# A mixture-of-experts layer: the shared expert's up products ahead of the expert loop, its down products behind it

## What is computed

```python
scores = softmax(xt @ router_w + router_b) + router_bias          # top 2 of 16, out of the best 2 of 4 groups
y = sum over the 16 experts of gate_e * ((silu(xt @ w1 + b1) * (xt @ w2 + b2)) @ w3 + b3)     # 512 -> 128 -> 512
z = silu(xt @ sw1 + sb1) * (xt @ sw2 + sb2) @ sw3 + sb3                                       # 512 -> 256 -> 512
out = x + y + z
```

## Time and profile before

| | |
|---|---|
| median of three runs | 253.63 us (250.83 to 255.41) |
| the profiled execution | 253.11 us, its span 251.4 us |
| busy: TensorE, VectorE, GpSimd, ScalarE | 240.5, 140.5, 110.1, 78.4 us |
| chain that ended last | TensorE 85%, VectorE 10% |
| granted clock of TensorE, mean | 0.993 |

### The profile page before, as it was taken

How to read it: one execution, slowest core, us unless ns; L and a number is a source line. 1 busy time by engine, 2 the same in 40 slices (tenths; PEclk the granted TensorE clock), 3 DMA queues, 4 the chain that set the end, 5 groups by cost and what they waited for, 6 DMA issues and landing times.

```text
span 251.4 us, 3931 instructions
## 1 busy us (share of the span) xinstructions
PE 240.5 (96%) x1092; PEld 162.8 (65%) x1093; DVE 140.5 (56%) x287; ACT 78.4 (31%) x169; POOL 110.1 (44%) x137
## 2 busy tenths in 40 slices
PE   7979999999999889999999999999999999999694
PEld 6847777888764446677777777777777644444231
DVE  0597876489799793333333333333333301698982
ACT  2345555222274002333333333333333311111400
POOL 6696665100200463666666666666663330000710
PEclk9999999999999999999999999999999999999979
DMA  6999998892449479754555444554553216999753
GB/s 198 343 415 404 369 317 304 296 372 59 197 154 417 183 197 330 266 169 168 167 167 167 126 156 135 167 167 167 167 167 125 89 57 232 391 387 389 303 207 126
DMA packets 20699, 57.91 MB, mean 230 GB/s; under 512 B 2533, under 2 KB 2533, under 8 KB 20428
## 3 DMA queue, kind: packets, MB, share of 16 engines
q1 hardware_dynamic: 15084, 39.89, 43.4%
q0 software_dynamic: 5600, 17.83, 21.5%
HBM read 40.94 MB, written 17.30 MB: 232 GB/s over the span
## 4 chain that ended last, share of the span: by engine, by line
PE 85%; DVE 10%; issue 2%; DMA 1%; ACT 0%; DVEq 0%
PE psum L586 76%; PE psum L732 6%; DVE xT L1214 3%; PE psum L629 2%; PE psum L745 2%; DVE xT L980 1%; DVE xT L954 1%; DMA xT<-cond_pack 1%; DVE x_early L954 1%; DVE r L954 1%; DVE xT L994 0%; DVE mix_bias L982 0%; DVE r L1170 0%; DVE code_f L1148 0%; DVE late_region L954 0%
## 5 line engine op out<-in xcount | busy, mean ns | idle before, releaser
L586 PE MATMUL psum<-wexp,r 128*128 x272 | 68.4, 381 | 0.4 <-DVE r L1170 0.3
L586 PEld LDWEIGHTS psum<-wexp,r 128*128 128x128 f32 x272 | 48.5, 190 | 22.8 <-issue 16.8
L954 DVE TENSOR_TENSOR r<-psum,ebias 128x256 f32<-128x256 f32 x34 | 14.4, 425 | 64.5 <-PE psum L586 64.5
L497 POOL DMA_INDIRECT expert_rows<-late_region,to_row x33 | 33.3, 1010 | 33.6 <-ACT late_region L897 33.6
L491 POOL DMA_INDIRECT late_region<-xt_rows,from_row x36 | 35.3, 980 | 16.9 <-issue 10.5
L586 PE MATMUL psum<-wexp,xt_sb 128*128 x68 | 34.8, 594 | 0.0
L586 PE MATMUL psum<-xT,shared_sb 128*128 128x512 f32 x64 | 28.0, 593 | 0.0
L891 ACT ACTIVATE r<-r 128x128 f32<-128x128 f32 x34 | 10.5, 309 | 55.3 <-DVE r L954 55.3
L897 ACT ACTIVATE late_region<-psum 128x512 f32<-128x512 f32 x34 | 20.3, 598 | 15.8 <-PE psum L586 15.8
L1170 DVE COPY r<-psum 128x512 f32<-128x512 f32 x36 | 24.5, 681 | 0.0
L732 PE MATMUL psum<-ident,late_region 128*128 128x128 f32 x144 | 21.6, 273 | 0.9 <-DMA late_region<-xt_rows,from_row 0.9
(11 more groups left out here) (177 smaller groups left out, 303.7 us busy)
## 6 DMA issues: line engine op xcount, KB each, us to landing
wexp<-expert_pack SPq DMA_DIRECT2D x16, 768.0 KB, 6.1
wexp<-expert_rows SPq DMA_DIRECT2D x8, 1024.0 KB, 12.9
xt_rows<-xt_sb SPq DMA_DIRECT2D x16, 256.0 KB, 4.7
x_early<-x SPq DMA_DIRECT2D x2, 1024.0 KB, 8.2
late_region<-x SPq DMA_DIRECT2D x2, 1024.0 KB, 12.8
ebias<-expert_bias SPq DMA_DIRECT2D x1, 2048.0 KB, 7.4
out_dram<-x_early SPq DMA_DIRECT2D x8, 256.0 KB, 9.8
shared_sb<-shared_pack SPq DMA_DIRECT2D x1, 1536.0 KB, 16.4
```

Of the source, the lines that this page charges most:

```text
L497: nc.gpsimd.indirect_dma_start(out=y_dram[:, :], out_offset=bass.IndirectOffsetOnAxis(ap=column.bitcast(U32), axis=0), in_=y_sb[:, slot, : ...
L586: return nc.tensor.matmul(dst, lhsT, rhs, start=start, stop=stop)
L954: return nc.vector.tensor_tensor(dst, a, b, op)
```

## The change

The shared expert's sixteen down products all move behind the expert loop, and its up products of groups 2 and 3 move ahead of it.

- **Up products.** All eight blocks are in split form. Groups 2 and 3 are split late into the memory of groups 0 and 1 (`late_splits`), by ScalarE between its SiLUs and by GpSimd between its gate subtractions. TensorE's order is: six blocks as the gates, ranks and splits allow, the seventh, the dispatch product, the eighth.
- **Weights of places 0 to 7.** Places 0 and 1 are loaded when group 2's blocks are done (`up_done` 6), the other six when all eight are (`up_done` 8). The loop no longer waits for both halves: SyncE raises `halves_ready` to 1 behind the six issues, when the first half is there, and to 2 when the second is; VectorE makes a table `tile_half` (1 or 2 for each tile), and `pe_step` loads its entry into a register and waits for `halves_ready` by it. SyncE issues the reloads of x between the two.
- **Tail.** TensorE makes the sixteen down products in the eight PSUM banks in turn, the last tile's own work between the first two. For tiles 0 to 3 and 15 VectorE adds z from PSUM; for tiles 4 to 14 ScalarE copies it to SBUF (`z_sb`) and GpSimd adds it. VectorE adds both rows of every tile, two tiles at a time, tiles 4 to 11 after GpSimd's addition, tiles 12 to 14 before it.

```diff
@@ sync
-                    sp.wait_ge(up_done, IB)
+                    sp.wait_ge(up_done, LAST * IB)
                 if place == FIRST_PLACES:
-                    sp.wait_ge(up_done, EARLY * IB)
+                    sp.wait_ge(up_done, NG * IB)
                 sp.dma_start(wexp[:, place, :], expert_pack[place]).then_inc(half_loaded[1], 16)
-            sp.wait_ge(down_done, EARLY * GT)
+            sp.wait_ge(half_loaded[0], 16 * (HALF + 1))
+            sp.sem_inc(halves_ready, 1)
             for t in range(EARLY * GT, NT):
                 sp.dma_start(acc_tile(t), x_rows[t * P:(t + 1) * P, :]).then_inc(x_again_loaded, 16)
+            sp.wait_ge(half_loaded[1], 16 * HALF)
+            sp.sem_inc(halves_ready, 1)
...
@@ gpsimd
+            def split_late(g):
+                for u in late_splits(g):
+                    pool.wait_ge(part_ready, u + 1)
+                    whole, part, rest = split_of(u)
+                    T.tensor_tensor(rest, whole, part, ALU.subtract).then_inc(split_ready, 1)
+            split_late(EARLY)
...
+            split_late(LAST)
...
-            for u in range(GT):
-                t = LAST * GT + u
-                pool.wait_ge(last_scaled, u + 1)
-                nc.gpsimd.tensor_tensor(acc_tile(t), acc_tile(t), rows_k[:, LAST, 1, u, :], op=ALU.add
-                                        ).then_inc(last_added, 1)
+            for t in range(Z_DVE, NT - 1):
+                pool.wait_ge(z_copied, t - Z_DVE + 1)
+                if t >= LAST * GT:
+                    pool.wait_ge(out_ready, t + 1)
+                T.tensor_tensor(acc_tile(t), acc_tile(t), z_sb[:, t - Z_DVE, :], ALU.add).then_inc(pool_z_ready, 1)
@@ tensor
-            shared_down(0)
-            shared_down(1, [0])
+            pe.wait_ge(split_ready, SPLITS + GT)
+            shared_up(2, 0)
+            shared_up(2, 1)
+            pe.wait_ge(split_ready, SPLITS + 2 * GT)
+            shared_up(3, 0)
             ... the dispatch product
-            shared_down(1, range(1, GT - 1))
+            shared_up(3, 1)
+            pe.wait_ge(up_ready, LAST * IB)
             pe.wait_ge(tables_ready, 1)
...
             def pe_step(i, b, slot, loaded):
                 n = i if isinstance(i, int) else 3
                 e = expert_of(i)
+                half = pe.value_load(tile_half[0:1, bass.ds(i, 1)], min_val=1, max_val=2)
+                pe.wait_ge(halves_ready, half)
                 pe.wait_ge(xgT_ready, i + 1)
                 if n == 0:
-                    pe.wait_ge(z_ready, EARLY * GT - 1)
+                    pe.wait_ge(up_ready, NG * IB)
                 up(b, e, 0)
...
-            pe.wait_ge(half_loaded[0], 16 * (HALF + 1))
-            pe.wait_ge(half_loaded[1], 16 * HALF)
...
-            shared_up(2, 0, between={(0, 1): lambda: hidden_transposed(1, tiles),
-                                     (0, 2): lambda: down(1, last_expert, tiles, tiles_less_2)})
-            shared_up(2, 1)
-            shared_up(3, 0)
-            shared_up(3, 1)
-            pe.wait_ge(y_ready, tiles)
-            shared_down(2)
-            shared_down(3)
+            shared_down_half(0, 0)
+            shared_down_half(0, 1)
+            hidden_transposed(1, tiles)
+            shared_down_bias(0)
+            pe.wait_ge(xgT_ready, tiles + 2)
+            shared_down_half(1, 0)
+            down(1, last_expert, tiles, tiles_less_2)
+            shared_down_half(1, 1)
+            shared_down_bias(1)
+            for t in range(2, NT):
+                if t == 6:
+                    pe.wait_ge(y_ready, tiles)
+                elif BANKS <= t < BANKS + Z_DVE:
+                    pe.wait_ge(first_z_ready, t - BANKS + 1)
+                elif t >= BANKS + Z_DVE:
+                    pe.wait_ge(z_copied, t - BANKS - Z_DVE + 1)
+                shared_down_half(t, 0)
+                shared_down_half(t, 1)
+                shared_down_bias(t)
@@ scalar
+            def split_late(g):
+                act.wait_ge(up_done, (g - EARLY + 1) * IB)
+                for u in late_splits(g):
+                    whole, part, _ = split_of(u)
+                    nc.scalar.activation(part, whole, ACT.Copy).then_inc(part_ready, 1)
...
+            for t in range(Z_DVE, NT - 1):
+                act.wait_ge(down_done, t + 1)
+                nc.scalar.activation(z_sb[:, t - Z_DVE, :], psum[:, t % BANKS, :], ACT.Copy).then_inc(z_copied, 1)
@@ vector
+            V.tensor_scalar(tile_half[:, :], code_f[:, :], float(HALF), 1.0, ALU.is_ge, ALU.add)
...
+            for t in range(Z_DVE):
+                add_z(t, first_z_ready)
+            dve.wait_ge(x_again_loaded, 16 * (NT - EARLY * GT))
+            for t in range(0, NT, 2):
+                g = t // GT
+                if t % GT == 0:
+                    dve.wait_ge(rows_loaded[g], 16 * TOPK)
+                for u in range(2):
+                    if g == 0:
+                        dve.wait_ge(first_z_ready, t + u + 1)
+                    elif g < LAST:
+                        dve.wait_ge(pool_z_ready, t + u - Z_DVE + 1)
+                    add_row(t + u, 0, row_added)
+                for u in range(2):
+                    dve.wait_ge(row_added, t + u + 1)
+                    add_row(t + u, 1, out_ready)
+            dve.wait_ge(out_ready, NT)
+            add_z(NT - 1, last_z_ready)
```

More of the change, by code:

```diff
@@ L157, in adaln_moe_ffn @@
         rows_k = wexp_flat[:, 0:NG * TOPK * GT * DIM].rearrange("p (g k t d) -> p g k t d", g=NG, k=TOPK, t=GT)
[L160 to L164, removed]
+        gs_last = xT[:, 0, IB:2 * IB, :]
+        z_sb = wexp_flat[:, NG * TOPK * GT * DIM:].rearrange("p (t d) -> p t d", d=DIM)
+        x_again = [xT[:, EARLY + u // C, u % C, :] for u in range(NT - EARLY * GT)]
         ident = sb("ident", [P, P])
@@ L327, in count_of, with late_splits @@
             return engine.value_load(tile_counts[0:1, n:n + 1], min_val=low, max_val=high)
[L329 to L333, removed]
+        def late_splits(g):
+            return range(SPLITS + (g - EARLY) * GT, SPLITS + (g - EARLY + 1) * GT)
         @block.sync
@@ L380, in _ @@
                                  ).then_inc(rows_loaded[g], 16)
-            for g in range(NG):
-                store_group(sp, g)
+            for t in range(NT):
+                if t < LAST * GT:
+                    sp.wait_ge(out_ready, t + 1)
+                elif t < NT - 1:
+                    sp.wait_ge(pool_z_ready, t - Z_DVE + 1)
+                else:
+                    sp.wait_ge(last_z_ready, 1)
+                sp.dma_start(out_rows[t * P:(t + 1) * P, :], acc_tile(t)).then_inc(out_stored, 16)
             sp.wait_ge(out_stored, 16 * NT)
@@ L651, in shared_up @@
                         cols = slice(i * P, (i + 1) * P)
-                        if g < EARLY:
-                            for n_product, (a, b) in enumerate(PRODUCTS):
-                                last = mm(psum[:, bank + w, :], w12_split[:, a, w, c, cols], x_split[:, g, b, c, :],
-                                          start=(c == 0 and n_product == 0),
-                                          stop=(c == C - 1 and n_product == len(PRODUCTS) - 1))
-                        else:
-                            last = mm(psum[:, bank + w, :], sw12[:, w, c, cols], xT[:, g, c, :],
-                                      start=(c == 0), stop=(c == C - 1))
@@ new lines, in shared_up, with shared_down_half @@
+                        for n_product, (a, b) in enumerate(PRODUCTS):
+                            last = mm(psum[:, bank + w, :], w12_split[:, a, w, c, cols],
+                                      x_split[:, g % EARLY, b, c, :], start=(c == 0 and n_product == 0),
+                                      stop=(c == C - 1 and n_product == len(PRODUCTS) - 1))
+                last.then_inc(up_done, 1)
+            def shared_down_half(t, i):
+                mm(psum[:, t % BANKS, :], gs_of(t // GT)[:, i, (t % GT) * P:(t % GT + 1) * P], sw3_sb[:, i, :],
+                   start=(i == 0), stop=False)
@@ L687, in _, with shared_down_bias @@
+            def shared_down_bias(t):
+                mm(psum[:, t % BANKS, :], gateT[:, t * P:(t + 1) * P], eb3x, start=False, stop=True
+                   ).then_inc(down_done, 1)
             pe.wait_ge(shared_loaded, 16)
```

130 lines of the change are left out of this document (43 added, 87 removed).

## The result

The changed kernel took 290.28 us in the median of its runs (289.41 to 292.19), the kernel before 254.52 beside it: 1.152 of it, 95% interval 1.137 to 1.167. A second set gave 291.28, ratio 1.152 (1.149 to 1.156). The forecast was 279, its range 261 to 287: the sign was right, the size 11 short and outside the range. The profiled execution is the longest of the four, 1.9 above their median. Its span is 290.4 against 251.4, +39.0: the loop starts at 108.0 instead of 93.0 (**+15.0**, forecast +11.6), lasts 129.0 instead of 107.0 (**+22.0**, forecast +17.1), and the tail takes 53.4 instead of 51.4 (**+2.0**, forecast -2.6).

A forecast was written before the change was run, and what follows sets the result against it. TensorE, 96% busy, was taken as the bound. Span 251.4+11.6 (front)+17.1 (loop)-2.6 (tail) = 277.5; with 1.7 outside the span 279.2, forecast 279 us, range 261 to 287.

The forecast's parts named there:

- Front: Ahead of the expert loop: its start, 93.0 before, comes later by 11.6 us (9.1 to 16.6).
- The wait behind SyncE's issues: Front: every tile waits for halves_ready behind six weight-load issues of 3.23 us; with 0.3 for release, first tile at 102.1.
- The meeting of GpSimd and VectorE: Front: group 2's four GpSimd subtractions slow VectorE's routing chain; at most 4.1 us, 0.8 taken.
- The clock: Front: idle stretches of TensorE lower its granted clock; 0 to 3.4 us lost, one fall of 1.7 taken.
- Loop: The 34 expert tiles, 107.0 us before: a second register load and a wait in each step add 17.1 (2.4 to 20.5).
- the row that is the very sequence: Loop: step 1's tile_counts load 0.65 before the expert's; the loop's load priced at 0.7, with the wait 0.8.
- Tail: Behind the loop, 51.4 us before: 48.8, so -2.6; -9.6 with no meeting, +1.4 if four more additions meet.
- VectorE's row additions: Tail: VectorE becomes the bound, 32 additions at 0.68, 1.0 lost per GpSimd meeting; last sum 46.3 us behind the tail's start.
- Store and end took 2.5 from there before: Tail: from VectorE's last sum out of PSUM to the end, 2.5 us as in the kernel before.
- (a): Loop: only the load itself counts, other sequencer work slips under TensorE; loop +2.4, 264.5 us; chance 0.12.
- (b): Loop: not slower, the sequencer works ahead and steps keep 3.14; 262.1 down to 252.6 us; chance 0.11.
- (c): Loop: the granted clock falls because of half a microsecond idle in each step; 290 us; chance 0.07.

The follow-up runs named there:

- the mends: Kernel after with half worked out in a register, first half released before SyncE's six issues, VectorE summing tiles 12 to 14: 264.17; also without group 2's subtractions: 261.63.
- the one in between: Three fixes to the kernel after, but group 3's up products behind the loop in plain form, group 2's ahead in split form: 269.53 us, ratio 1.064.

## Why the prediction was right in sign and short in size

The sum of the three terms is 12.9 short in the execution shown. The range stopped at 287, although the bounds given for the terms add up to 291.6 (251.4+16.6+20.5+1.4+1.7): the front lies inside its bounds, the loop 1.5 and the tail 0.6 above theirs. And 279.2 with 0.5 for the median is 279.7, not 279.

**Front, 3.4 short.** *The wait behind SyncE's issues*: right in place; they took 4.20 where the earlier trace rows gave 3.23, so that 4.6 instead of 3.5 passed from the last block to the first tile (1.1 short). But the step was too simple: transposes and VectorE's copy lie under it, and without it 3.3 would be left. *The meeting of GpSimd and VectorE*: I took 0.8 of 0 to 4.1, because the first subtraction would come late in the chain. It came at 62.30, ahead of the operations that it slowed, and the block started 2.7 late (1.9 short); without the subtractions it starts at 75.85, and at 74.91 with the mends besides. *The clock*: four blocks and the dispatch product took 25.9 for 23.7, 2.2 where I had 1.7. Group 3's subtractions, at nothing, held narrowly: they took 9.96 us instead of 5.1, from 77.29 to 87.25, and TensorE didn't wait.

**Loop, 4.9 short: the largest miss.** By the hidden transposes the 22.0 are 13.3 for the load at 0.30 (119.2 without scatters against 105.9 without the load), 5.7 for its meeting with the scatter, 0.6 between 105.9 and before, and 2.4 before the first transpose (5.9 from the first product, 3.5 before), 1.8 of that the clock. The mechanism held: queue time on TensorE's sequencer that matmuls no longer cover, and most where the branch stands. The load alone was even taken too high (17.1 for 13.3), so that the loop is no more than 4.9 short is in part luck: two errors of opposite sign. The step that failed is the price by "the row that is the very sequence": step 1 has no scatter beside it, and in the loop the load meets one and takes 0.51. And of two falls of the clock that the front allowed for I took one; both came, the second at the loop's start. The Trainium skill (Runtime: NRT & Kernel Launch, Instruction fetch mechanics) gives a register load about 200 ns, as an uncached round trip, and speaks of loads that the runtime puts in. The runs have 0.30 alone and medians of 0.51 to 0.55 with the scatters, so its figure is no bound here.

**Tail, 4.6 short, with the wrong sign.** *VectorE's row additions* were right: 16x0.68+5 was 15.9 forecast for the first 16 and 15.75 came, with five meetings of 1.0 each; the last 16 weren't slowed (16 in 10.68), where two meetings were forecast. *"Store and end took 2.5 from there before"* is the step that failed: 8.9 passed from VectorE's last addition to the end. I followed the engine that I had named the bound and not the one with the last work. GpSimd's addition of tile 12 lay 4.29 us beside VectorE's chain, 3.0 of them lost; VectorE wasn't slowed. And GpSimd's program ends 5.8 us behind its last addition, which the earlier trace rows couldn't show, since its last addition there ended at 240.0 and the closing was hidden. With VectorE adding these tiles 2.7 pass, near the 2.5, and the tail is 4.6 shorter. The Trainium skill (SBUF — State Buffer, SBUF: two separate sides) describes the two engines' common port as a lock held for a whole instruction while the other stands still. The 4.29 beside VectorE's 0.74 agrees with the standing still; that four of VectorE's additions pass a waiting GpSimd is more than one instruction's lock.

**Rivals.** (a) and (b) fell: steps of 3.78. (c) was right in kind: a falling clock at the loop's start, but for the first 6 us and behind the wait in front of the loop, not for idle time in its steps; from 114 on the clock was full again.

## What to carry to other kernels

An instruction that waits for nothing and computes nothing still costs its time where a queue has no slack: count the slack for each kind of step, and price the instruction by a row that has the same neighbours, not the same form. A number that a register already yields shouldn't be loaded: one register instruction in place of the load gave back 19 us. And follow each engine to the end of its own program, not only the one that bounds the stage.

## What the runs showed of the hardware that was not expected

- A register load of TensorE's queue takes 0.30 us alone; in the kernel after 20 of 34 take 0.50 to 0.58, while a scatter's transfer moves. Without scatters 34 of 34 take at most 0.318.
- A semaphore wait against a register, ahead of each step, costs nothing that can be measured (277.65 with it, 277.93 without).
- GpSimd's closing DRAIN ends 5.82 us behind its last addition in every version that gathers and scatters all its tiles: 284.4 to 290.2 after, 264.1 to 269.9 with VectorE's sums, and 240.0 to 245.8 before. It goes with the number of those transfers: with all 70 it is 5.82, without most gathers (38 left) 3.21, without most scatters (37 left) 3.13. By these three each adds 0.082 us, an estimate. The DRAIN rows of the kernel before, without gathers and without scatters (the last additions of these two end at 285.28 and 278.95):

```profile
L59 POOLq DRAIN  x1: 10249/10249/10249, 235.6 to 235.6; - x1
...
L59 POOLq DRAIN  x1: 7314/7314/7314, 281.2 to 281.2; - x1
...
L59 POOLq DRAIN  x1: 7232/7232/7232, 274.8 to 274.8; - x1
```

- The branch out of the loop's code took 3.0 to 3.3 us of TensorE's queue in three versions (both with the load in the kernel before, and the one in between) and 0.21 to 0.44 in the others; why is open.
